# Values right behind scores, turns of probabilities in odd slots, a mask in 64x32 blocks, rope tables one by one

## The chip, the cores and the metric

The kernel runs on one core of a Trainium2 chip. The metric is the device time of one execution in microseconds (us). The engines are TensorE (PE in the profile, its weight loads PEld), VectorE (DVE), ScalarE (ACT), GpSimd (POOL) and SyncE (SP), which issues the transfers. Each engine works through its own queue in order; semaphores tie the queues together.

## The reference

The input is x of 16 sequences x 256 tokens x 128 features, f32. First comes a selective state space block (the first 18% of the span), which the change doesn't touch. Then `x + ffn(layernorm(x))`, where ffn is six layers of local attention and a gated feed-forward part:

```python
for i in range(DEPTH):                       # 6
    x = attn_layer(shift_tokens(x), Wqkv[i], q_scale[i], k_scale[i], Wo[i]) + x
    x = ffn_layer(shift_tokens(x), ln_g[i], ln_b[i], W1[i], b1[i], W2[i], b2[i]) + x
```

The attention has 16 heads of 64. q and k are normalised to length one per head, scaled by a vector, and turned by rotary tables. The sequence is cut in windows of 32 tokens. The queries of a window see its own 32 keys and the 32 before it; of these 64 keys, those later than the query or more than 32 earlier are masked, and the first window of a sequence has no earlier keys. Softmax over the 64 keys, then the weighted sum of v, then the product with Wo. The feed-forward part is a layer norm, a product to 2 x 341, `a * gelu(gate)`, and a product back to 128.

## The kernel before

All is f32, except the mask and its identity (bf16). x stays in SBUF, turned (features on partitions), in `xT`.

**Slots.** A layer is 64 slots (`LAYER`). Slot k begins unit k: one sequence has four units, two chunks of 128 tokens times q and k. Every engine runs the same function `layer_slot(l, k)` for each slot, with its own part of the work, and each kind of work has a lag: unit t's rope is in slot t, its turn to `qT` or `kT` in slot t + 2. A layer's tail overlaps with the next layer's head, in a loop over layers. `step_at` gives work that comes once in two slots, a step: half the heads of a sequence. There are 192 steps. Scores have lag 6, sums of the exponentials 7, turn of the probabilities (`LAG_PTURN`) 8, values (`LAG_VALUES`) 9, output product (`LAG_OUT`) 10, addition to x 11. So scores, turn of probabilities and output product lie in even slots, values and addition in odd ones. `group_at` gives feed-forward work, once per eight slots (48 groups in all): mean 19, variance 21, up products 23, 25 and 27, down product 29; all in odd slots. In k % 8 these are: 3 the mean and up products; 5 the variance and the down product; 7 up products with two Gelus; 1 up products with one Gelu.

**TensorE, one slot** (`layer_slot`, L1225 to L1297), in this order: the unit's projection into `QK` (L1130); feed-forward products (L1215, L1222, L1238, L1250); scores of a step (L1158, L1164); first turn of unit k - 2, `transposes(..., 0)` (L1002); values (L1188); in even slots the projection of v into `VOB` (L1136); turn of the probabilities into `OB` (L1002); second turn of unit k - 2; in odd slots the projection of v; output product into `VOB` (L1196). A line `trb L1002` in the profile is a first or second turn, `ob L1002` the turn of the probabilities.

**The mask** is written into the PSUM tile `SC` by two bf16 products of the full array, an identity times the mask repeated over the head pairs (L1158); the scores are added on top (L1164), each a block of 64 rows by 32 columns of the array. Values are blocks of 64 by 64 (L1188), 128 matmul instructions per step, as the scores.

**What TensorE waits for.** Both turns of a unit go through one PSUM bank, `TRB`: the second waits until ScalarE has copied the first away (`tr_evac`, L633). Mean, variance, v and output product all use `VOB`: the output product waits for ScalarE's copy of v (`v_ready`, L640) and of the values (`o_evac`, L656); v in an odd slot waits for VectorE's use of the mean (`ln_xc`, L956), ScalarE's logarithm (`ln_log`, L703), or the addition to x (L919).

**ScalarE, one slot** (L680): squares of the unit (L619); table load and Gelus (L686, L678); copy of the first turn; the feed-forward norm's square, logarithm and exponential (L698, L703, L705); copy of the values (`out_evac`, L656); in even slots copy of v (L640); copy of the turned probabilities (`probs_evac`, L649); copy of the second turn; in odd slots copy of v; table load back (L721); in slots k % 4 = 2 staging of x (L663 to L671); exponentials of a step (L644); the unit's norms (L623, L626).

**VectorE, one slot** (L934): addition to x (L919), sums (L910), rope (L889, L890), maxima and subtraction (L902, L905), feed-forward operations (L956, L925, L931), sums of squares (L895, L897), norm (L976, L979). At a layer's first slot `layer_tables` makes the four rope tables (L878).

**GpSimd**: divides the probabilities (L514), adds the halves of the rope (L500), scales a unit (L507). **SP** loads weights and shifts copies of v by half a block (`vs` from `vn`).

Of the kernel before, what the change touches and what calls it, by code (L numbers as in the profile page):

```python
# [12 lines left out]
P = 128  # L13
# [3 lines left out]
CHUNKS = SEQ // P  # L17
D_INNER, D_STATE, CONV = 256, 16, 4
MT = D_INNER // P
DEPTH, HEADS, HEAD, WINDOW = 6, 16, 64, 32  # L20
# [17 lines left out]


LAG_TURN, LAG_V, LAG_SHIFT = 2, 3, 4  # L40
LAG_SCORES, LAG_SUM, LAG_PTURN, LAG_VALUES, LAG_OUT, LAG_ADD = 6, 7, 8, 9, 10, 11
LAG_STAGE, LAG_MEAN, LAG_VAR, LAG_NORMED = 17, 19, 21, 22
LAG_UP, LAG_DOWN = (23, 25, 27), 29
TURN = 32
# [52 lines left out]
def build(nc, t, out):  # L97
# [3 lines left out]
    with ctx:  # L101
# [5 lines left out]
        def sem(name, credits=0):  # L107
            s = ctx.enter_context(nc.semaphore(name))
            credit[name] = credits
            return (s, credits)  # L110

        def item(e, s, n):

            e.wait_ge(s[0], n + (1 + s[1]))
# [183 lines left out]
        vproj_done = sem("vproj_done", 2 * UNITS)  # L298
        v_ready = sem("v_ready", 1)
        vs_in = sem("vs_in")  # L300
        s_done = sem("s_done", 2 * STEPS)
        mx_done = sem("mx_done")
        sub_done = sem("sub_done", 1)
# [226 lines left out]
        def _(act_e):  # L530
# [142 lines left out]
            def gelu(group, n, m, done, col):  # L673
                h0, hn = HT[m]
                act_e.wait_ge(up_done[0], n * (2 * NHT) + done + 1)
                if m == 0:
                    slot(act_e, y_done, n)
                A(gl(group, m)[0:hn], SC[0:hn, col:col + 512], ACT.Gelu, bias=lpar[0:hn, 3 + NHT + m:4 + NHT + m]).then_inc(gelu_done[0], 1)  # L678

            def layer_slot(l, k):  # L680
                unit = unit_at(l, k, 0)
                if unit:
                    squares(*unit)
                up0, up1 = group_at(l, k, LAG_UP[0]), group_at(l, k, LAG_UP[1])
                if up0 or up1:
                    act_e.preload_act_table(ACT.Gelu)  # L686
                if up0:
                    gelu(*up0, 0, 0, 0)
                    gelu(*up0, 1, 1, 512)
                if up1:  # L690
                    gelu(*up1, 2, 2, 0)
                at_ = unit_at(l, k, LAG_TURN)
                if at_:
                    turned(*at_, 0)
                at_ = group_at(l, k, LAG_MEAN)
                if at_:
                    item(act_e, ln_xc, at_[1] + 2 * GROUPS)
                    A(sq2[0], xc[0], ACT.Square).then_inc(ln_sq[0], 1)  # L698
                at_ = group_at(l, k, LAG_VAR)
                if at_:  # L700
                    item(act_e, ln_var, at_[1] + 2 * GROUPS)
                    item(act_e, ln_out, at_[1] + (2 * GROUPS - 1))
                    A(rstd[0], bank[2][:], ACT.Ln, bias=eps[:, 0:1]).then_inc(ln_log[0], 1)  # L703
                    item(act_e, ln_log, at_[1] + 2 * GROUPS)
                    A(rstd[0], rstd[0], ACT.Exp, scale=-0.5).then_inc(ln_rstd[0], 1)  # L705
                at_ = step_at(l, k, LAG_VALUES)
                if at_:
                    out_evac(*at_)
                value = v_at(l, k)
                if value and k % 2 == 0:  # L710
                    v_evac(value[0], value[3:], value[2])
                at_ = step_at(l, k, LAG_PTURN)
                if at_:
                    probs_evac(*at_)
                at_ = unit_at(l, k, LAG_TURN)
                if at_:
                    turned(*at_, 1)
                if value and k % 2:
                    v_evac(value[0], value[3:], value[2])
                if up0 or up1:  # L720
                    act_e.preload_act_table_set(EXP_LN_SET)  # L721
                if k % UNITS == 2:
                    at_ = unit_at(l, k, -2)
                    if at_:
                        stage_x(at_[1], at_[2], (k + 2) // UNITS % BATCH, l + (k + 2) // LAYER)
                    at_ = group_at(l, k - 1, LAG_STAGE)
                    if at_:
                        stage_norm(*at_)
                at_ = step_at(l, k, LAG_SCORES)
                if at_:  # L730
                    exps(*at_)
                if unit:
                    norms(*unit)
# [17 lines left out]
        def _(dve):  # L751
# [119 lines left out]
            item(dve, mo_used, GROUPS - 1)  # L871
            plain_norm(GROUPS, xT)

            def layer_tables(l, layer):

                for c in range(CHUNKS):
                    for tab, base, sc in ((tab_q, base_q, scale_q), (tab_k, base_k, scale_k)):
                        V.tensor_tensor(tab[:, c], base[:, c], sc[:, ds(layer, 1), :].to_broadcast([P, 2, HEAD]), ALU.mult) \  # L878
                            .then_inc(tabs_done[0], 1)

            def rope(U, B, u, c, j):

# [51 lines left out]
            def layer_slot(l, k):  # L934
                at_ = step_at(l, k, LAG_ADD)
                if at_:
                    add_x(*at_, (k - LAG_ADD) // UNITS % BATCH * SEQ)
                at_ = step_at(l, k, LAG_SUM)
                if at_:
                    sums(*at_)  # L940
                unit = unit_at(l, k, 0)
                if unit and k % LAYER == 0:
                    layer = l + k // LAYER
                    if k:
                        item(dve, roped, unit[0] * 2 + -1)
                    layer_tables(l, layer)
                    item(dve, tabs_done, layer * (2 * CHUNKS) + (2 * CHUNKS - 1))
                if unit:
                    rope(*unit)
                at_ = step_at(l, k, LAG_SCORES)  # L950
                if at_:
                    maxima(*at_)
                at_ = group_at(l, k, LAG_MEAN)
                if at_:
                    item(dve, ln_mean, at_[1] + 2 * GROUPS)
                    V.tensor_tensor(xc[0], xs2.rearrange("p s t -> p (s t)"), bank[2][:], ALU.subtract).then_inc(ln_xc[0], 1)  # L956
                at_ = group_at(l, k, LAG_UP[1])
                if at_:
                    hidden(*at_, 0, 3, 512)
                at_ = group_at(l, k, LAG_UP[2])  # L960
                if at_:
                    hidden(*at_, 1, 4, 0)
                    hidden(*at_, 2, 5, 512)
                at_ = group_at(l, k, LAG_DOWN)
                if at_:
                    add_y(*at_)
                if unit:
                    square_sums(*unit)
                at_ = group_at(l, k, LAG_NORMED)
                if at_:  # L970
                    if at_[0] == 0:
                        layer = l + (k - LAG_NORMED) // LAYER
                        V.tensor_copy(lpar[:], lpar_all[:, ds(layer, 1), :].rearrange("p o n -> p (o n)")).then_inc(lpar_done[0], 1)
                        item(dve, lpar_done, layer)
                    item(dve, ln_rstd, at_[1] + 2 * GROUPS)
                    V.scalar_tensor_tensor(out=xc[0], in0=xc[0], scalar=lpar[:, 0:1], in1=rstd[0], op0=ALU.mult, op1=ALU.mult) \  # L976
                        .then_inc(ln_aff[0], 1)
                    item(dve, ln_aff, at_[1])
                    V.tensor_scalar(xnT[:, at_[0] * GROUP:at_[0] * GROUP + GROUP], xc[0], lpar[:, 1:2], None, ALU.add).then_inc(ln_out[0], 1)  # L979

            dve.wait_ge(lpar_in[0], N_LPAR)
            dve.wait_ge(cleared[0], 2)
            item(dve, ln_out, 2 * GROUPS - 1)
            layer_slots(dve, layer_slot)
            item(dve, x_next, DEPTH * GROUPS - 1)
# [10 lines left out]
        def _(pe):  # L996
# [147 lines left out]
            def scores(s, B, u, j, n, up0, up1, up2, down):  # L1144
# [9 lines left out]
                    pe.wait_ge(hid_done[0], up2[1] * NHT + 3)  # L1154
                if down:
                    item(pe, x_next, down[1])
                for h in range(2):
                    MM(SC[:, 512 * h:512 * h + 512], lhsT=ident16[:], rhs=mask[:, :].unsqueeze(1).to_broadcast([P, STEP_PAIRS, 2 * SPAN]),  # L1158
                       start=True, stop=True)
                for a in range(STEP_PAIRS):  # L1160
                    for b, g, t0 in windows():
                        for h in range(2):
# [62 lines left out]
            def layer_slot(l, k):  # L1225
# [30 lines left out]
                at_ = step_at(l, k, LAG_SCORES)  # L1256
                if at_:
                    scores(*at_, *(group_at(l, k - 1, lag) for lag in LAG_UP), group_at(l, k - 1, LAG_DOWN))
                turned = unit_at(l, k, LAG_TURN)
                if turned:  # L1260
                    transposes(*turned, 0)
                at_ = step_at(l, k, LAG_VALUES)
                if at_:
                    values(*at_)
                value = v_at(l, k)
                if value and (k - LAG_V) % LAYER == 0:
                    pe.wait_ge(wqkv_in[2][0], (l + (k - LAG_V) // LAYER) * 16 + 16)
# [49 lines left out]
def constants():  # L1317
# [5 lines left out]

    i, k = np.arange(P)[:, None], np.arange(2 * SPAN)[None, :]
    inside = (k % SPAN >= i % WINDOW) & (k % SPAN <= i % WINDOW + WINDOW)
    inside &= (i >= WINDOW) | (k >= SPAN) | (k % SPAN >= WINDOW)
    out["mask"] = np.where(inside, 0.0, MASKED).astype(bf)

    sel = np.zeros((P, 2 * D_STATE, P))
# [36 lines left out]
```

## Time and profile before

| | |
|---|---|
| three runs | 3815.24, 3816.27 (median), 3817.18 us |
| profiled execution | 3817.41 us, span 3815.5 us |
| PE busy | 3549.1 us, 93% |
| DVE busy | 3112.5 us, 82% |
| ACT busy | 2650.5 us, 69% |
| POOL busy | 2420.8 us, 63% |
| transfers | 120.05 MB, some 11% of the 16 DMA engines |

A timeline row is a run of like instructions: start, the time from the first start to the last end, and their count. Matmuls are pipelined, so runs overlap, and the distance from one row's start to the next row's start is what a run takes of TensorE's time. An f32 product is recorded as two matmuls. A share of busy time is an average over all stages.

### The profile page before, as it was taken

The page shows a single profiled execution, that of the slowest core. Times are in us where ns is not written, and L with a number is a line of the kernel's source. Part 1 is how long each engine was busy: PE and PEld are TensorE (multiplying, and loading weights), DVE is VectorE, ACT ScalarE, POOL GpSimd, SP SyncE. Part 2 cuts the span into 40 slices and gives each one's busy share as a digit, 9 for nine tenths or more (in the row PEclk, how much of TensorE's full clock was granted, in tenths as well). Part 3 has the DMA queues.
Part 4 walks back from the last instruction along what each step waited for, and adds up shares of the span by engine and source line. Part 5 has one row for each costly group of instructions (what it writes and reads, how often), then busy time and mean ns, then how long its engine had stood idle before and what let it go on. Part 6 is the DMA issues. An engine that isn't in the chain of part 4 may idle for free.

```text
span 3815.5 us, 146379 instructions
## 1 busy us (share of the span) xinstructions
PE 3549.1 (93%) x60112; PEld 2231.2 (58%) x60128; DVE 3112.5 (82%) x4377; ACT 2650.5 (69%) x4972; POOL 2420.8 (63%) x2197
## 2 busy tenths in 40 slices
PE   5667676899999999999999999999999999999997
PEld 2222222466666666666666666666666666666664
DVE  4899998888888888888878888878888788888884
ACT  3545454677777777777777777777777777777775
POOL 0356555776666666666666666666666666666661
PEclk9889899999999999999999999999999999999999
DMA  3000000010111111111111111111111111111101
GB/s 78 0 0 0 0 0 0 26 37 28 33 35 48 37 33 32 32 48 37 37 33 32 43 43 35 30 32 32 48 41 34 32 32 48 37 37 29 33 28 38
DMA packets 64418, 120.05 MB, mean 31 GB/s; under 512 B 18196, under 2 KB 35986, under 8 KB 63634
## 3 DMA queue, kind: packets, MB, share of 16 engines
q1 hardware_dynamic: 63762, 110.70, 10.0%
q8 instruction: 485, 7.95, 0.9%
q14 instruction: 171, 1.40, 0.1%
HBM read 20.50 MB, written 2.10 MB: 6 GB/s over the span
## 4 chain that ended last, share of the span: by engine, by line
PE 79%; issue 2%; DVE 2%; ACT 1%; POOL 0%; DMA 0%; ACTq 0%; POOLq 0%; DVEq 0%; SPq 0%
PE qk L1130 17%; PE trb L1002 10%; PE ob L1188 10%; PE vob L1196 8%; PE vob L1136 8%; PE sc L1164 7%; PE sc L1215 6%; PE ob L1002 4%; PE sc L1222 3%; PE sc L1158 2%; PE vob L1238 1%; PE vob L1250 1%; DVE arena L889 0%; DVE ssq L895 0%; DVE arena L890 0%
## 5 line engine op out<-in xcount | busy, mean ns | idle before, releaser
L507 POOL TENSOR_TENSOR arena<-arena,rnorm 128x512 f32<-128x512 f32 x768 | 785.2, 1044 | 930.0 <-ACT rnorm L626 929.5
L500 POOL TENSOR_TENSOR arena<-arena 128x512 f32<-128x512 f32 x768 | 962.8, 1275 | 35.9 <-DVE arena L890 35.9
L633 ACT ACTIVATE arena<-trb 128x512 f32<-128x512 f32 x768 | 462.6, 602 | 441.6 <-PE trb L1002 441.6
L1130 PE MATMUL qk<-wqkv,xs 128*128 128x512 f32 x1536 | 729.4, 597 | 16.3 <-issue 9.2
L889 DVE TENSOR_TENSOR arena<-qk,tab_q 128x512 f32<-128x512 f32 x384 | 263.3, 686 | 455.0 <-ACT arena L619 447.6
L483 POOL TENSOR_TENSOR arena<-arena 128x512 f32<-128x512 f32 x256 | 300.0, 1182 | 346.4 <-DVE arena L859 333.8
L1002 PE MATMUL trb<-ident,arena 128*128 128x128 f32 x3072 | 482.3, 280 | 9.8 <-ACT arena L633 7.3
L1130 PEld LDWEIGHTS qk<-wqkv,xs 128*128 128x128 f32 x1536 | 292.7, 191 | 309.1 <-issue 291.7
L895 DVE TENSOR_REDUCE ssq<-arena 128x16 f32<-128x1024 f32 x384 | 463.7, 1207 | 0.0
L619 ACT ACTIVATE arena<-qk 128x512 f32<-128x512 f32 x768 | 426.8, 588 | 45.0 <-PE qk L1130 28.1
L1002 PEld LDWEIGHTS trb<-ident,arena 128*128 128x128 f32 x3072 | 346.7, 141 | 140.1 <-issue 88.3
L514 POOL TENSOR_TENSOR arena<-arena,rinv 128x512 f32<-128x512 f32 x384 | 392.6, 1044 | 23.1 <-DVE rinv L912 23.1
L1188 PE MATMUL ob<-arena 64*64 64x32 f32 x24576 | 397.2, 220 | 0.0
L1188 PEld LDWEIGHTS ob<-arena 64*64 64x64 f32 x24576 | 375.9, 135 | 33.9 <-issue 33.9
L1136 PE MATMUL vob<-wqkv,xs 128*128 128x512 f32 x768 | 393.8, 594 | 1.1 <-DVE arena L956 1.1
L1196 PE MATMUL vob<-arena,wo 128*128 128x256 f32 x1536 | 363.6, 380 | 1.3 <-ACT arena L656 1.3
L1164 PEld LDWEIGHTS sc<-arena 64*32 64x32 f32 x24576 | 254.7, 105 | 84.3 <-issue 84.2
L1196 PEld LDWEIGHTS vob<-arena,wo 128*128 128x128 f32 x1536 | 276.9, 190 | 31.2 <-issue 1.4
L1164 PE MATMUL sc<-arena 64*32 64x64 f32 x24576 | 287.0, 225 | 1.5 <-issue 1.1
L1215 PE MATMUL sc<-xnT,w 128*128 128x512 f32 (+1 forms) x576 | 271.1, 593 | 5.3 <-DVE xnT L979 2.2
L640 ACT ACTIVATE arena<-vob 128x512 f32<-128x512 f32 x384 | 232.9, 607 | 51.1 <-PE vob L1136 50.8
L1090 PE MATMUL sc<-arena,ident 128*128 128x512 f32 x512 | 257.3, 624 | 8.8 <-POOL arena L483 6.8
(139 smaller groups left out, 5879.6 us busy)
## 6 DMA issues: line engine op xcount, KB each, us to landing
arena<-arena SPq DMA_DIRECT2D x192, 384.0 KB, 3.2
arena<-arena SPq DMA_DIRECT2D x192, 64.0 KB, 3.0
wqkv<-in_L_ffn_Wqkv SPq DMA_DIRECT2D x18, 512.0 KB, 4.6
wo<-in_L_ffn_Wo SPq DMA_DIRECT2D x6, 512.0 KB, 4.0
arena<-in_L_attn_x SPq DMA_DIRECT2D x8, 256.0 KB, 2.9
out<-arena SPq DMA_DIRECT2D x8, 256.0 KB, 2.2
w<-in_L_ffn_W SPq DMA_DIRECT2D x6, 341.0 KB, 2.9
arena<-in_sel SPq DMA_DIRECT2D x1, 1024.0 KB, 5.0
```

What stands on the lines that cost most here:

```text
L500: nc.gpsimd.tensor_tensor(ts[c * 2 + j][:, heads], tu[:, 0, heads], tu[:, 1, heads], ALU.add).then_inc(summed[0], 1)
L507: nc.gpsimd.tensor_tensor(part, part, rnorm[j][:, 8 * h:8 * h + 8].unsqueeze(2).to_broadcast([P, 8, HEAD]), ALU.mult) \
L619: A(sq[j][:, cols], QK[:, cols], ACT.Square).then_inc(sq_ready[0], 1)
L633: A((qT, kT)[j][u][:, 4 * h:4 * h + 4, at_col:at_col + P], TRB.rearrange("p (a t) -> p a t", a=4), ACT.Copy) \
L895: V.tensor_reduce(ssq[j][:], sq[j].rearrange("p (h e) -> p h e", h=HEADS), op=ALU.add, axis=AX.X).then_inc(ssq_done[0], 1)
L1002: return MM(out_, lhsT=in_, rhs=ident[0:k, 0:k], is_transpose=True, **kw)
L1130: MM(QK[:, 512 * h:512 * h + 512], lhsT=xs[u][:, c * P:(c + 1) * P], rhs=wqkv[:, col:col + 512], start=True, stop=True) \
L1136: MM(VOB[:, :], lhsT=xs[u][:, c * P:(c + 1) * P], rhs=wqkv[:, col:col + STEP_COLS], start=True, stop=True).then_inc(vproj_done[0], 1)
L1164: last = MM(SC[32 * g:32 * g + 32, col:col + SPAN], lhsT=qT[u][d, STEP_PAIRS * j + a, t0:t0 + WINDOW], rhs=kT[u][d, STEP_PAIRS * j + a, t0 ...
L1188: last = MM(OB[d, col:col + WINDOW], lhsT=v[keys, g // 2, (2 * a + h) * HEAD:(2 * a + h + 1) * HEAD], rhs=probT[keys, h, a, g * WINDOW:(g ...
L1196: last = MM(VOB[:, 0:SEQ], lhsT=wo[:, STEP_PAIRS * j + a, :], rhs=oT[:, a, :], start=a == 0, stop=a == STEP_PAIRS - 1)
L1215: MM(SC[0:hn, 512 * b:512 * b + 512], lhsT=w1[:, col:col + hn], rhs=rhs, start=True, stop=True).then_inc(up_done[0], 1)
```

## The change

Turn of the probabilities has lag 9 and values lag 10: the turn now lies in odd slots, the values in even ones, where TensorE does them right behind the scores of a later step and ahead of the first turn. ScalarE's copy of the values comes accordingly right behind the squares and Gelus, ahead of the copy of the first turn. The mask is written by eight products of 64x32 blocks, behind a new semaphore increment; the mask constant is repeated in both halves of the partitions. The four rope tables of a layer are made one at a time, behind the last units that use the old one, and each of the first four units of a layer waits for its own.

```diff
-LAG_SCORES, LAG_SUM, LAG_PTURN, LAG_VALUES, LAG_OUT, LAG_ADD = 6, 7, 8, 9, 10, 11
+LAG_SCORES, LAG_SUM, LAG_PTURN, LAG_VALUES, LAG_OUT, LAG_ADD = 6, 7, 9, 10, 10, 11
...
@@ ScalarE
                 if up1:
                     gelu(*up1, 2, 2, 0)
+                at_ = step_at(l, k, LAG_VALUES)
+                if at_:
+                    out_evac(*at_)
                 at_ = unit_at(l, k, LAG_TURN)
                 if at_:
                     turned(*at_, 0)
...
-                at_ = step_at(l, k, LAG_VALUES)
-                if at_:
-                    out_evac(*at_)
                 value = v_at(l, k)
...
@@ VectorE
-            def layer_tables(l, layer):
-
-                for c in range(CHUNKS):
-                    for tab, base, sc in ((tab_q, base_q, scale_q), (tab_k, base_k, scale_k)):
-                        V.tensor_tensor(tab[:, c], base[:, c], sc[:, ds(layer, 1), :].to_broadcast([P, 2, HEAD]), ALU.mult) \
-                            .then_inc(tabs_done[0], 1)
+            def layer_table(layer, c, j):
+
+                tab, base, sc = (tab_q, tab_k)[j], (base_q, base_k)[j], (scale_q, scale_k)[j]
+                V.tensor_tensor(tab[:, c], base[:, c], sc[:, ds(layer, 1), :].to_broadcast([P, 2, HEAD]), ALU.mult).then_inc(tabs_done[0], 1)
...
-                if unit and k % LAYER == 0:
-                    layer = l + k // LAYER
-                    if k:
-                        item(dve, roped, unit[0] * 2 + -1)
-                    layer_tables(l, layer)
-                    item(dve, tabs_done, layer * (2 * CHUNKS) + (2 * CHUNKS - 1))
+                if unit and k % LAYER < UNITS:
+                    dve.wait_ge(tabs_done[0], (l + k // LAYER) * UNITS + k % LAYER + 1)
...
+                ahead = unit_at(l, k, 1)
+                if ahead and not isinstance(l, int) and LAYER - UNITS <= (k - 1) % LAYER:
+                    item(dve, roped, ahead[0] * 2 + 1)
+                    layer_table(l + 1, ahead[3], ahead[4])
...
@@ TensorE
-                for h in range(2):
-                    MM(SC[:, 512 * h:512 * h + 512], lhsT=ident16[:], rhs=mask[:, :].unsqueeze(1).to_broadcast([P, STEP_PAIRS, 2 * SPAN]),
-                       start=True, stop=True)
+                pe.sem_inc(s_open[0], 1)
+                for g in range(4):
+                    for h in range(2):
+                        d, pick = slice(64 * h, 64 * h + 64), 64 * h + (WINDOW if g else 0)
+                        MM(SC[32 * g:32 * g + 32, 512 * h:512 * h + 512], lhsT=ident16[d, pick:pick + WINDOW],
+                           rhs=mask[d, :].unsqueeze(1).to_broadcast([64, STEP_PAIRS, 2 * SPAN]), start=True, stop=True, skip_group_check=True)
...
                 if at_:
                     scores(*at_, *(group_at(l, k - 1, lag) for lag in LAG_UP), group_at(l, k - 1, LAG_DOWN))
+                at_ = step_at(l, k, LAG_VALUES)
+                if at_:
+                    values(*at_)
                 turned = unit_at(l, k, LAG_TURN)
                 if turned:
                     transposes(*turned, 0)
-                at_ = step_at(l, k, LAG_VALUES)
-                if at_:
-                    values(*at_)
...
-    inside &= (i >= WINDOW) | (k >= SPAN) | (k % SPAN >= WINDOW)
+    inside &= (i % SPAN >= WINDOW) | (k >= SPAN) | (k % SPAN >= WINDOW)
```

## Rows read from the trace of the kernel before

**Rows 1.** Of the page: busy time of the engines; shares of the chain of waits

```profile
PE 3549.1 (93%) x60112; PEld 2231.2 (58%) x60128; DVE 3112.5 (82%) x4377; ACT 2650.5 (69%) x4972; POOL 2420.8 (63%) x2197
...
PE 79%; issue 2%; DVE 2%; ACT 1%; POOL 0%; DMA 0%; ACTq 0%; POOLq 0%; DVEq 0%; SPq 0%
```

**Rows 2.** One stretch of 2800 us in the layers: time, busy per engine, TensorE clock, DMA

```profile
900.00:3700.00 2800.00, 2789.58 (x53631) 1857.29 (x53632) 2286.88 (x3290) 2093.62 (x4007) 1919.47 (x1742) 1.00 0.13 36
```

**Rows 3.** Waits of TensorE in that stretch: us in total, times, longest

```profile
PE qk L1130 <- issue: 9.2, 4, 2.5
```

**Rows 4.** TensorE in order of time, an even slot: start us, us, instructions

```profile
2007.92 1.88 PE L1130 MATMUL qk<-wqkv,xs 128*128 128x512 f32 x4
2009.64 0.59 PE L1158 MATMUL sc<-mask,ident 128*128 128x512 bf16 x2
2010.16 1.48 PE L1164 MATMUL sc<-arena 64*32 64x64 f32 x128
2011.58 0.65 PE L1002 MATMUL trb<-ident,arena 128*128 128x128 f32 x4
2012.07 1.02 PE L1136 MATMUL vob<-wqkv,xs 128*128 128x512 f32 x2
2012.93 1.04 PE L1002 MATMUL ob<-ident,arena 128*128 128x128 f32 x8
2013.80 0.60 PE L1002 MATMUL trb<-ident,arena 128*128 128x128 f32 x4
2014.24 1.89 PE L1196 MATMUL vob<-arena,wo 128*128 128x256 f32 x8
2015.97 1.88 PE L1130 MATMUL qk<-wqkv,xs 128*128 128x512 f32 x4
```

**Rows 5.** TensorE in order of time, the odd slot that follows

```profile
2020.26 0.60 PE L1002 MATMUL trb<-ident,arena 128*128 128x128 f32 x4
2020.79 2.07 PE L1188 MATMUL ob<-arena 64*64 64x32 f32 x128
2022.79 0.66 PE L1002 MATMUL trb<-ident,arena 128*128 128x128 f32 x4
```

**Rows 6.** Groups by shape: busy us, mean ns | idle before us

```profile
L889 DVE TENSOR_TENSOR arena<-qk,tab_q 128x512 f32<-128x512 f32 x384 | 263.3, 686 | 455.0 <-ACT arena L619 447.6 <-POOL arena L500 7.4
...
L1158 PE MATMUL sc<-mask,ident 128*128 128x512 bf16 x384 | 114.2, 379 | 0.2 <-DVE hid_last L925 0.2
...
L878 DVE TENSOR_TENSOR tab_k<-base_k,scale_k 128x128 f32<-128x128 f32 x12 | 3.3, 279 | 0.0
```

**Rows 7.** TensorE in order of time, in the tail of the last layer

```profile
3769.91 2.07 PE L1188 MATMUL ob<-arena 64*64 64x32 f32 x128
3773.28 1.97 PE L1196 MATMUL vob<-arena,wo 128*128 128x256 f32 x8 [1.30 <-ACT arena L656]
```

**Rows 8.** ScalarE in order of time, the same place in the tail

```profile
3772.05 1.08 ACT L656 ACTIVATE arena<-ob 128x512 f32<-128x512 f32 x2 [1.34 <-PE ob L1188]
```

**Rows 9.** TensorE in order of time, start of an odd slot with two Gelus

```profile
2049.27 1.88 PE L1130 MATMUL qk<-wqkv,xs 128*128 128x512 f32 x4
```

**Rows 10.** ScalarE in order of time, that odd slot and its end

```profile
2051.81 1.28 ACT L686 ACT_TABLE_LOAD   x1
...
2054.26 0.60 ACT L633 ACTIVATE arena<-trb 128x512 f32<-128x512 f32 x1
2055.44 1.09 ACT L656 ACTIVATE arena<-ob 128x512 f32<-128x512 f32 x2 [0.59 <-PE ob L1188]
2056.41 0.60 ACT L633 ACTIVATE arena<-trb 128x512 f32<-128x512 f32 x1
2056.89 0.62 ACT L640 ACTIVATE arena<-vob 128x512 f32<-128x512 f32 x1
```

**Rows 11.** VectorE in order of time, the odd slot of rows 5

```profile
2022.15 0.67 DVE L956 TENSOR_TENSOR arena<-xs,vob 128x512 f32<-128x512 f32 x1
```

**Rows 12.** ScalarE in order of time, the even slot of rows 4

```profile
2014.58 0.62 ACT L633 ACTIVATE arena<-trb 128x512 f32<-128x512 f32 x1
```

More of the change, by code:

```diff
@@ L300, in build @@
         vs_in = sem("vs_in")
+        s_open = sem("s_open")
         s_done = sem("s_done", 2 * STEPS)
@@ L982, in _ @@
             dve.wait_ge(cleared[0], 2)
+            for c in range(CHUNKS):
+                for j in range(2):
+                    layer_table(0, c, j)
             item(dve, ln_out, 2 * GROUPS - 1)
```

## The prediction

> **What bounds the kernel now.** I read the page's totals first. TensorE is busy 93% of the span, the next engine 82%, and 79% of the chain that ended last is TensorE [rows 1]. A share over all stages says little, so the second view is one stretch inside the layers. There TensorE is busy 2789.6 of 2800 us at a granted clock of 1.00, which is the 2.4 GHz level; VectorE has 2286.9 and ScalarE 2093.6 [rows 2]. The third view, the waits of TensorE there, has 9.2 us in four waits of up to 2.5 us [rows 3]. So the layers are a gapless stream of TensorE: whatever shortens it is gained in full, and every new wait in it is paid in full. The other engines' slack matters only as distance to the next TensorE instruction that waits for them. That distance is read from the timelines, as start-to-start times (busy times overlap). Two slots make one step; there are 192 steps, in 48 groups of eight slots.
>
> An even slot, from S = 2007.92, issues projection 1.72, mask 0.52, scores 1.42, first turn 0.49, values projection (v) 0.86, probabilities' turn 0.87, second turn 0.44, output product 1.73: 8.05 us [rows 4]. In the odd slot first turn 0.53 and values 2.00 follow the feed-forward products [rows 5].
>
> **Gain 1, the mask.** Two blocks of 512 bf16 columns take 0.59 in all and one takes 0.379, so the second starts 0.21 behind the first; 0.52 less two of these leaves 0.09 before the first 64x32 block [rows 4, 6]. The same 0.09 is the difference between the turn ahead of values (0.53) and the one ahead of the output product (0.44) [rows 4, 5]. After the change the 0.09 stands ahead of the mask, and eight blocks on eight parts of the array stream the 512 columns. No row has such a block. Below: side by side, 0.21, no less, for one part must still stream 512 columns. Above: the four blocks of one half one after another, 0.86. The nearest row is the 128 score blocks on the same eight parts: 1.42/128 = 11 ns each, of 64 f32 columns, where 512 take 0.43 and so 64 take 54 ns [rows 4]. They clearly run side by side, and I take 0.21. Mask and entry go from 0.52 to 0.31: 0.21 x 192 = 41 us. The upper end would make it a loss of 0.43 x 192 = 83 us.
>
> The Trainium skill, "TensorE: Matmul & The Clock Gate", Measured speedup vs the span model, gives 6.32x for nine packed blocks, some 70% of nine. By that, as an estimate, the eight blocks would take about 0.30 and the gain would be 18 us less; the score rows show overlap but do not separate 70% from 100%.
>
> **Gain 2, one change of block shape fewer.** Values are no longer entered from a full-array turn, so 0.09 goes: x 190 steps = 17 us. What stands between the last score block and the first value block no row shows: nothing (then 0.05 more gained) up to one more 0.09 (nothing gained). I take the exit that the turn behind scores has now, already inside 1.42.
>
> The Trainium skill, "TensorEngine Tiling (Array Packing)", Key Properties, says a change of tiling mode drains the array; the 0.09 at every entry agrees. 64x32 to 64x64 would be such a change, which is the value taken.
>
> **No gain or loss.** The table edit moves 24 operations of about 0.28 us on VectorE [rows 6]. VectorE idles 447.6 us in all before the q rope, waiting for ScalarE's squares, which hides them at either place [rows 6]; without that cover they would cost 24 x 0.28 = 7 us. The added semaphore increment ahead of the mask: the same kind stands ahead of values, whose entry costs the same 0.09 as the scores' without one, so nothing (at most 0.1 x 192 = 19 us). Turning probabilities one slot later frees `prob` one slot later, but the subtraction that rewrites it stands a slot behind that turn. Value buffers come free one slot later; four steps apart, the copy that waits for them comes in the slot after. No DMA moves; SP's shifts hang on that copy and have a slot more before values.
>
> **Loss 1, behind values in every even slot.** Now the probabilities' turn and the second turn, 1.31 us, stand between v and the output product; afterwards only the second turn, 0.44. Count from the start of values, B. Ideal: first turn B+2.00, v B+2.49, second turn B+3.35, output product B+3.79. ScalarE must first copy the two halves of values, for it is now first in its queue. It starts 0.07 behind values' end (3769.91 + 2.07 to 3772.05) [rows 7, 8], B+2.14, and a copy follows the other every 0.485 (2055.44 to 2056.41 for two), each ending 0.60 after its start [rows 10]. So: copy of the first turn B+3.11 to B+3.71, copy of v B+3.59 to B+4.20 (v itself ends B+2.49 + 1.02 = B+3.51). The second turn needs the bank that the first copy frees (`tr_evac`), the output product the bank of v (`v_ready`). TensorE restarts 0.15 behind such a copy (3773.13 to 3773.28), its block then 0.08 longer (1.97 against 1.89) [rows 4, 7, 8]. Output product in effect B+4.42 against 3.79: 0.63. Without restart cost it is 0.41. Queued behind it: the next projection, so the whole stream. I take 0.63 x 189 = 119 us.
>
> **Loss 2, odd slots whose length was the cover.** They lose values (2.00) and gain a turn (0.87). From the slot's start T, first turn after projection and up products 3.44, second turn due at T+3.44+0.44+0.87 = 4.75.
> - With two Gelus, T = 2049.27: table load 2051.81, copy of the first turn 2054.26 to 2054.86, T+5.59 [rows 9, 10]. All of it hangs on this slot's projection, so it stays. The second turn waits until 5.69 (0.1 taken for the restart): 0.94.
> - With one Gelu the copy is 0.57 earlier (two Gelus and a load fill 2051.81 to 2054.26, the load 1.28): T+5.02, so 0.37.
> - With the mean, T = 2015.97: v overwrites the mean's bank and waits for the subtraction, which ends 2022.82, T+6.85 [rows 4, 11]. It hangs on ScalarE's second copy in the slot before, now 1.39 ahead of T (2014.58) [rows 12], after the change 1.65 (second turn's copy B+4.49, T at B+6.14), so T+6.59. v is due at T+4.29+0.44+0.87+0.44 = 6.04 [rows 4, 5]: 0.65 with the restart.
> - With the variance: about 0.1, v against the logarithm.
>
> Some 46 of the 48 groups have these slots full: (0.94 + 0.37 + 0.65 + 0.1) x 46 = 95 us. With the restarts at nothing: 0.84, 0.27, 0.55 and 0 make 76.
>
> **The sum.** Gains 41 + 17 = 58; losses 119 + 95 = 214; net +156. The profiled execution took 3817.4 (its span 3815.5), so 3973; the median of the runs is 1.1 lower: 3972 us. In slots: eight took 64.1, they would take 67.3. Own range: losses 77 + 76 give 3911; mask at 0.30, and a second shape change's 17 give 4007.
>
> **Rivals.**
> 1. Only Loss 1: ScalarE's and VectorE's chains in the short odd slots move forward with them. For: with the long even slot both engines have more time in all. Against: the table load hangs on the slot's own projection. 3816 - 58 + 119 = 3877. Chance 0.12.
> 2. The mask blocks of one half run one after another. For: no row has bf16 blocks of 512 columns there. Against: 11 ns a score block. 3972 + 124 = 4096. Chance 0.07.
> 3. Faster: the copies behind values don't hold TensorE. Place: `v_ready` and `tr_evac` in the even slot; price 0.63; it decides where the waits of a step sum to under 58/192 = 0.30 us. For: the stream has no wait there now. Against: v ends 0.28 before the output product is due and its copy lasts 0.6. 3816 - 58 = 3758. Chance 0.08.
> 4. Gains and losses cancel, with half of each loss. 3816. Chance 0.03.
>
> The forecast has 0.70. The range 3865 to 4012 takes in rival 1. A measurement of this kernel tells 0.2% (8 us) from no change: faster 0.08, same 0.03, slower 0.89.
>
> **What would show it.** In the waits of TensorE, the second turn and the output product waiting for ScalarE's copies, about 0.4 to 0.6 in each even slot, and a wait of v for VectorE's subtraction once a group; these rows hardly exist now. Mask to scores start-to-start 0.21 with eight blocks. Values right behind scores in the timeline, at the old 2.00. Wrong if: the output product starts within 0.1 of the second turn's end; a slot of two Gelus lasts under 6.2 us; or the mask block lasts over 0.4.

## The result and the profile after

The changed kernel takes 4456.6 us (median of 4 runs, 4448.9 to 4460.4) against 3816.7: 1.167 times as long, interval 1.166 to 1.169. The prediction said 3972: it had the direction right and the size wrong, +156 us forecast and +640 measured. The profiled execution's span is 4454.8 us.

The page after, its totals, the chain of waits, two groups by shape and the queue that brings instructions:

```profile
PE 3800.4 (85%) x61280; PEld 2348.5 (53%) x61280; DVE 3097.2 (70%) x4377; ACT 2648.5 (59%) x4972; POOL 2418.3 (54%) x2197
...
q8 instruction: 492, 8.06, 0.8%
...
PE 60%; issue 15%; ACT 8%; DVE 3%; POOL 0%; ACTq 0%; DMA 0%; DVEq 0%; POOLq 0%; SPq 0%
...
L1193 PE MATMUL ob<-arena 64*64 64x32 f32 x24576 | 458.8, 224 | 282.9 <-issue 280.8
...
L1138 PE MATMUL vob<-wqkv,xs 128*128 128x512 f32 x768 | 479.1, 711 | 11.4 <-DVE arena L951 11.3
```

"issue" went from 2% of the chain [rows 1] to 15%. It is time in which TensorE does nothing and the profile shows nothing that it waits for. 280.8 us of it lie inside the values (now L1193). The last row is another loss: one matmul of the v product lasts 711 ns on average, where it lasted 594.

The waits of TensorE between 1000 and 4300 us (total, times, longest); before, the same view of the layers had a single row of 9.2 us [rows 3]:

```profile
PE ob L1193 <- issue: 249.7, 160, 2.9
PE trb L1004 <- ACT arena L634: 67.9, 164, 0.8
PE qk L1132 <- issue: 10.7, 4, 2.8
PE vob L1138 <- DVE arena L951: 8.7, 25, 0.5
PE vob L1201 <- ACT arena L641: 7.8, 27, 0.3
```

TensorE in order of time, an even slot whose clock stays at the upper level, answering to [rows 4]:

```profile
2109.54 1.88 PE L1132 MATMUL qk<-wqkv,xs 128*128 128x512 f32 x4
2111.35 0.41 PE L1163 MATMUL sc<-mask,ident 64*32 64x512 bf16 x8
2111.58 1.46 PE L1169 MATMUL sc<-arena 64*32 64x64 f32 x128
2112.98 1.00 PE L1193 MATMUL ob<-arena 64*64 64x32 f32 x52
2115.26 1.35 PE L1193 MATMUL ob<-arena 64*64 64x32 f32 x76 [1.27 <-issue]
2116.54 0.66 PE L1004 MATMUL trb<-ident,arena 128*128 128x128 f32 x4
2117.04 1.02 PE L1138 MATMUL vob<-wqkv,xs 128*128 128x512 f32 x2
2118.35 0.65 PE L1004 MATMUL trb<-ident,arena 128*128 128x128 f32 x4 [0.29 <-ACT arena L634]
2118.84 1.99 PE L1201 MATMUL vob<-arena,wo 128*128 128x256 f32 x8
2120.67 1.88 PE L1132 MATMUL qk<-wqkv,xs 128*128 128x512 f32 x4
```

The mask takes 0.23 us from start to start and values begin 1.40 behind the scores, as worked out. Then values stop after 52 of their 128 instructions for more than a microsecond, with no semaphore in between. Behind them second turn and output product are late, nearly as forecast: from the first turn to the output product it is 2.30 us, where the forecast had 2.42 (B+2.00 to B+4.42) and 1.79 without waits. The slot lasts 11.13 us; forecast 9.6. ScalarE's copies in that slot (of the first turn, of v):

```profile
2117.62 0.60 ACT L634 ACTIVATE arena<-trb 128x512 f32<-128x512 f32 x1
2118.10 0.62 ACT L641 ACTIVATE arena<-vob 128x512 f32<-128x512 f32 x1
```

They end at 2118.22 and 2118.72; the second turn and the output product start 0.13 and 0.12 behind. Nearly all of the delay is the second turn's: the output product starts 0.49 behind it, where it started 0.44 behind it before [rows 4].

TensorE in an odd slot with two Gelus, and the start of the next:

```profile
2083.05 1.88 PE L1132 MATMUL qk<-wqkv,xs 128*128 128x512 f32 x4
2084.76 1.88 PE L1220 MATMUL sc<-xnT,w 128*128 128x512 f32 x4
2086.48 0.60 PE L1004 MATMUL trb<-ident,arena 128*128 128x128 f32 x4
2086.92 1.04 PE L1004 MATMUL ob<-ident,arena 128*128 128x128 f32 x8
2088.76 0.66 PE L1004 MATMUL trb<-ident,arena 128*128 128x128 f32 x4 [0.80 <-ACT arena L634]
2089.25 1.02 PE L1138 MATMUL vob<-wqkv,xs 128*128 128x512 f32 x2
2090.11 0.59 PE L1132 MATMUL qk<-wqkv,xs 128*128 128x512 f32 x1
```

The second turn starts 5.71 us into the slot; forecast 5.69. The slot lasts 7.06; forecast 6.99.

**Where the values stop.** Three things can be counted in the trace. First, in program order of TensorE's instructions, the 180 stops of over 0.6 us in scores and values lie multiples of 256 apart, nearly always 512, 768 or 1280; a third are off by one, four by seven. Second, the queue `q8 instruction` brings one piece of 16 KB at a time, 492 in all, which is a piece for some 256 instructions of TensorE. In the slot above one starts at 2112.92 and lands at 2113.88, and values go on at 2115.26, 1.37 us behind the landing; over all of these stops this distance is 1.2 to 1.6 us, median 1.38. Third, from the instruction 256 ahead of a stop's end to that end it is 3.5 us in the median, and 3.1 to 4.3 in nine of ten. So in this kernel a piece becomes usable some 3.5 us after TensorE has entered the piece before it. Scores and values are 256 instructions each (128 weight loads, 128 matmuls) at 5.5 and 7.2 ns apiece: a piece is used up in 1.7 us, and 1.8 are missing. There are 175 stops of over 0.25 us inside values, together 315 us.

In the kernel before, eight such stops stand inside scores, 3.2 us in all. The only one of over 0.6 us from start to start is in the tail, where a slot's other work is gone (TensorE in order of time; 0.58 us of it idle):

```profile
3752.88 0.76 PE L1164 MATMUL sc<-arena 64*32 64x64 f32 x52
3754.22 0.99 PE L1164 MATMUL sc<-arena 64*32 64x64 f32 x76 [0.58 <-issue]
```

**The clock.** Another even slot, in which TensorE's clock fell; then the two slots and the odd one behind them as windows (stretch, length, busy per engine, granted clock, DMA):

```profile
2131.73 1.83 PE L1193 MATMUL ob<-arena 64*64 64x32 f32 x112
2135.10 0.43 PE L1193 MATMUL ob<-arena 64*64 64x32 f32 x16 [1.53 <-issue]
2135.47 0.66 PE L1004 MATMUL trb<-ident,arena 128*128 128x128 f32 x4
2135.96 1.80 PE L1138 MATMUL vob<-wqkv,xs 128*128 128x512 f32 x2
2137.56 1.06 PE L1004 MATMUL trb<-ident,arena 128*128 128x128 f32 x4
```

```profile
2109.54:2120.67 11.13, 9.57 (x287) 6.92 (x286) 6.33 (x9) 6.94 (x14) 4.64 (x5) 1.00 0.08 22
2128.30:2139.88 11.58, 10.05 (x283) 6.83 (x282) 7.75 (x11) 6.40 (x14) 5.86 (x6) 0.85 0.05 12
2139.88:2147.86 7.98, 7.98 (x35) 4.72 (x33) 5.92 (x9) 3.06 (x8) 6.54 (x6) 1.00 0.16 47
```

In the second slot v lasts 1.80 instead of 1.02: the lower of the two levels, 1.2 GHz (a granted clock of 0.50 from 2136.07 to 2139.48), behind a stop in the values that ended at 2135.10. Of the 102 stretches at the lower level in the layers, 95 begin inside a stop or within 3 us behind one, which together is a quarter of the layers' time. Of the 176 even slots that have every kind of work, 86 run at the upper level throughout and last 11.22 us on average, with 1.49 us of stops; 90 have a stretch at the lower level and last 12.96, with 1.85 us of stops.

### The profile page after: what moved, and what is told of

It is laid out like the page before. It is cut to its first block, busy times and chain, and to the rows that moved or that the text cites. A ratio compares the mean times of both kernels' runs of the same rounds, so it can differ in the third digit from the quotient of the medians.

```text
span 4454.8 us, 148907 instructions
## 1 busy us (share of the span) xinstructions
PE 3800.4 (85%) x61280; PEld 2348.5 (53%) x61280; DVE 3097.2 (70%) x4377; ACT 2648.5 (59%) x4972; POOL 2418.3 (54%) x2197
## 4 chain that ended last, share of the span: by engine, by line
PE 60%; issue 15%; ACT 8%; DVE 3%; POOL 0%; ACTq 0%; DMA 0%; DVEq 0%; POOLq 0%; SPq 0%
PE qk L1132 14%; PE ob L1193 10%; PE vob L1138 8%; PE trb L1004 8%; PE vob L1201 7%; PE sc L1169 6%; PE sc L1227 3%; ACT arena L634 2%; PE sc L1163 1%; PE ob L1004 1%; PE sc L1220 1%; PE vob L1243 1%; ACT L687 1%; DVE arena L889 1%; DVE rsum L909 1%
## 5 line engine op out<-in xcount | busy, mean ns | idle before, releaser
L1193 PE MATMUL ob<-arena 64*64 64x32 f32 x24576 | 458.8, 224 | 282.9 <-issue 280.8
L657 ACT ACTIVATE arena<-ob 128x512 f32<-128x512 f32 x384 | 208.4, 595 | 787.9 <-PE ob L1193 787.9
L1004 PE MATMUL trb<-ident,arena 128*128 128x128 f32 x3072 | 549.1, 306 | 89.1 <-ACT arena L634 80.2
L1004 PEld LDWEIGHTS trb<-ident,arena 128*128 128x128 f32 x3072 | 387.1, 154 | 427.2 <-issue 357.6
L1193 PEld LDWEIGHTS ob<-arena 64*64 64x64 f32 x24576 | 417.9, 139 | 311.9 <-issue 294.8
L1138 PE MATMUL vob<-wqkv,xs 128*128 128x512 f32 x768 | 479.1, 711 | 11.4 <-DVE arena L951 11.3
L918 DVE TENSOR_TENSOR xT<-vob,xT 128x256 f32<-128x256 f32 x192 | 81.5, 424 | 574.6 <-PE vob L1201 574.4
L1201 PE MATMUL vob<-arena,wo 128*128 128x256 f32 x1536 | 408.0, 411 | 13.9 <-ACT arena L641 9.0
L1201 PEld LDWEIGHTS vob<-arena,wo 128*128 128x128 f32 x1536 | 297.0, 205 | 83.0 <-issue 35.9
L1169 PEld LDWEIGHTS sc<-arena 64*32 64x32 f32 x24576 | 279.5, 105 | 18.0 <-issue 7.3
```

The source lines that it names most:

```text
L1004: return MM(out_, lhsT=in_, rhs=ident[0:k, 0:k], is_transpose=True, **kw)
L1138: MM(VOB[:, :], lhsT=xs[u][:, c * P:(c + 1) * P], rhs=wqkv[:, col:col + STEP_COLS], start=True, stop=True).then_inc(vproj_done[0], 1)
L1169: last = MM(SC[32 * g:32 * g + 32, col:col + SPAN], lhsT=qT[u][d, STEP_PAIRS * j + a, t0:t0 + WINDOW], rhs=kT[u][d, STEP_PAIRS * j + a, t0 ...
L1193: last = MM(OB[d, col:col + WINDOW], lhsT=v[keys, g // 2, (2 * a + h) * HEAD:(2 * a + h + 1) * HEAD], rhs=probT[keys, h, a, g * WINDOW:(g ...
L1201: last = MM(VOB[:, 0:SEQ], lhsT=wo[:, STEP_PAIRS * j + a, :], rhs=oT[:, a, :], start=a == 0, stop=a == STEP_PAIRS - 1)
```

## The experiments

Two theories stood. F: the stops are the supply of instructions; they need more than 256 short instructions in a row. S: they come from values standing directly behind scores with another block shape. A third, C, puts the loss on ScalarE's copies and the clock, and M, in one expectation, on the mask blocks. The first four kernels ran together; their time before was 3820.3 us. The old order and values first have four runs each, the tables alone eleven, and every other kernel a single one; stops are counted in the trace of one run each.

**The old order, mask blocks and single tables kept.**

```diff
-LAG_..., LAG_PTURN, LAG_VALUES, LAG_OUT, LAG_ADD = 6, 7, 9, 10, 10, 11
+LAG_..., LAG_PTURN, LAG_VALUES, LAG_OUT, LAG_ADD = 6, 7, 8, 9, 10, 11
# and values, out_evac back in their old places
```

> The changed kernel with the old order put back (turn of probabilities lag 8, values lag 9 in odd slots behind the first turn, copy of the values in its old place); mask blocks and single rope tables stay. Theory F (instruction supply): TensorE's instructions arrive in pieces of 256; a piece is ready about 3.5 us after TensorE enters the one before, so 256 score instructions with 256 value instructions right behind run dry at a piece's boundary. Here 256 short instructions stand alone, so no gap over 0.6 us inside values, and the mask's gain stays: 0.21 x 192 = 41 us, 3775 us (3768 to 3788). Rival M (the mask blocks are the cause): even slots stay over 10 us, 4200 us or more. Rival S (the cause is values standing directly behind scores with another block shape): 3775 too.

Measured 3787.6 us (3784.3 to 3791.7), ratio 0.991, interval 0.989 to 0.993: 33 us faster than before. Its TensorE, in an even slot:

```profile
2010.79 1.88 PE L1132 MATMUL qk<-wqkv,xs 128*128 128x512 f32 x4
2012.60 0.41 PE L1163 MATMUL sc<-mask,ident 64*32 64x512 bf16 x8
2012.83 1.46 PE L1169 MATMUL sc<-arena 64*32 64x64 f32 x128
2014.22 0.66 PE L1004 MATMUL trb<-ident,arena 128*128 128x128 f32 x4
```

From the projection to the first turn it is 3.43 instead of 3.66 [rows 4]. The mask blocks don't cause the loss (M falls), and this kernel beats both others. The whole loss is in the order.

**Half of the values.**

```diff
-                for a in range(STEP_PAIRS):        # values
+                for a in range(STEP_PAIRS // 2):
```

> The changed kernel with only half of the value products (pairs 0 and 1 of 4; leaves the other half of the attention's output wrong). 384 short instructions in a row in place of 512. Theory F: a whole piece of 256 lies inside the row only where its boundary falls in the first 128, so the gap is in about half of the 192 steps (80 to 115, against 175 now), each still some 1.8 us; time about 3972 - 0.93 x 190 = 3795, plus 95 x 1.8 = 171, plus up to 60 for the clock: 3940 to 4030. Rival S (change of shape right behind scores): a gap in every step, 4456 - 176 = 4280. Rival C (the copies of ScalarE and the lower clock, no supply): no gaps inside values, 3800 to 3900.

Measured 4018.1 us, inside F's range. Stops inside values: 96, together 159 us, where there were 175. The half that F worked out from 384 against 256 is met; a stop at every meeting of scores and values (S) and no stop (C) fall.

**Scores twice in the kernel before.**

```diff
-                for a in range(STEP_PAIRS):        # scores
+                for a in 2 * list(range(STEP_PAIRS)):
```

> The kernel before with every score product issued twice (scores come out doubled), so 512 short instructions of one shape stand in a row; order, mask and values as before. Theory F: a gap inside the scores in nearly every step, 3.5 - 1.4 = 2.1 us: 3816 + 192 x 1.35 (259) + 190 x 2.1 (399) = 4475 us (4350 to 4600). Rivals S and C: no gap, 3816 + 259 = 4075 us.

Measured 4502.2 us, inside F's range; the rivals had 4075. TensorE in one of its even slots (the view begins inside the row), its waits, and the instruction queue:

```profile
2099.77 1.59 PE L1164 MATMUL sc<-arena 64*32 64x64 f32 x140
2103.52 0.86 PE L1164 MATMUL sc<-arena 64*32 64x64 f32 x65 [2.15 <-issue]
```

```profile
PE sc L1164 <- issue: 306.7, 166, 3.7
```

```profile
q8 instruction: 677, 11.09, 1.0%
```

These are 169 stops inside scores, 344 us in all, with no values near, no change of shape and no late copy: neither S nor C can explain them. The 192 x 256 instructions more bring 192 pieces more (677 against 485).

**Values at the head of the even slot.**

```diff
 def layer_slot(l, k):
+    values(*at_)        # TensorE; on ScalarE out_evac ahead of the squares
     unit(*unit_)
     scores(...)
-    values(*at_)
```

> The changed kernel with values (and ScalarE's copy of them) moved to the head of the even slot, ahead of the unit's projection: 1.72 + 0.31 us of long products now stand between the 256 value and the 256 score instructions. Theory F: gaps shrink to under 0.3 us, even slots to about 9.7, and the time falls to what the waits of the prediction leave: 3985 us (3950 to 4050). Rival S: 3985 as well. Rival C (values in an even slot cost what they cost wherever they stand in it): over 4300 us.

Measured 4265.4 us (4262.4 to 4269.4), ratio 1.117, interval 1.115 to 1.119. F and S said 3985, C over 4300: a miss, and nearer to C. The waits of TensorE between 1000 and 4000 us:

```profile
PE ob L1193 <- issue: 69.6, 45, 4.4
PE ob L1193 <- ACT arena L650: 57.2, 82, 0.8
PE sc L1169 <- issue: 36.5, 32, 2.0
PE vob L1201 <- ACT arena L641: 31.8, 149, 0.3
```

Two things were left out of the expectation. Values now wait for ScalarE's copy of the turned probabilities from the slot before. And 52 stops in values and 48 in scores, together 133 us, are left of the changed kernel's 175 and 11, though no row has more than 256 short instructions. F said gaps under 0.3 us, and that is wrong.

The trace shows where F is too simple. At the stops of over 0.6 us the time from the instruction 256 ahead to the stop's end is no longer 3.5 us but 5.4 in the median and up to 11.8. The distance from a piece's landing to going on is still 1.2 to 1.6 us; it is the fetch that starts late, 2.9 us in the median behind the entry into the piece before, where it was 1.0 in the changed kernel, and often only when TensorE is already in the short row. So the start of a fetch is not a fixed time behind that entry. What sets it stays open, and so does the part of the 280 us over the expectation that stops and waits don't fill.

The next four ran together, before at 3817.1 us.

**Half of scores and half of values, new and old order.** The two edits of above, once in the changed kernel and once in the old order with mask blocks.

> The changed kernel with half of the score products and half of the value products (leaves the attention's output wrong): values still right behind scores, but 256 short instructions in all, no longer than one piece. Theory F: hardly a gap, the clock stays at its upper level, and the time is the forecast's: 3972 less 0.66 x 190 for scores and 0.93 x 190 for values, 3670 us (3640 to 3710), with the output product waiting for the copies 0.6 us in each even slot. Theory C (clock and copies make the loss, supply little): the same loss as now, 4456 - 302 = 4154 us.

> The old order with mask blocks (the kernel e1_old_order) with the same half of scores and values left out. 3788 - 302 = 3486 us, and some 50 us of waits in odd slots, since values' 1.0 us less there uncovers the copy of the first turn (0.7 us with two Gelus) and v's wait for the mean's subtraction: 3510 to 3550. The difference to e8_half_both_new, 130 us (100 to 170), is what the reordering costs without the supply. Theory C: the difference is some 600 us.

Measured 3734.2 and 3692.6 us; both are above their ranges. In the new order there are 11 stops, 6 us, where 175 were: 256 short instructions in a row, though scores and values still touch. The lower clock goes with them: 8 stretches of it in the layers against 102. The even slot lasts 8.03 us in the median; the forecast less the work left out, 9.60 - 1.59, is 8.01. TensorE there (second turn and output product late by the copies):

```profile
2100.30 0.66 PE L1004 MATMUL trb<-ident,arena 128*128 128x128 f32 x4
2100.79 1.02 PE L1138 MATMUL vob<-wqkv,xs 128*128 128x512 f32 x2
2102.14 0.65 PE L1004 MATMUL trb<-ident,arena 128*128 128x128 f32 x4 [0.32 <-ACT arena L634]
2102.63 1.99 PE L1201 MATMUL vob<-arena,wo 128*128 128x256 f32 x8
```

The difference of the two is 42 us, not 130. Both expectations were too low: with so much work gone TensorE waits for other engines in the odd slots. In the new order the four odd slots of a group last 0.7 us longer than in the changed kernel; in the old order with half of the work these waits of TensorE between 1000 and 3600 us are new (with all products no wait of that view for VectorE or ScalarE stands there):

```profile
PE sc L1220 <- DVE xnT L978: 68.6, 42, 1.9
PE trb L1004 <- ACT arena L634: 49.5, 42, 1.3
PE vob L1138 <- DVE arena L951: 19.1, 42, 0.5
```

So the pair shows that stops and lower clock all but vanish with the row of short instructions, and doesn't show what the order alone costs.

**The projection of v between scores and values; then first turn and v between.**

```diff
     scores(...)
+    v_unit(...)         # second kernel: transposes(*turned, 0), then v_unit(...)
     values(*at_)
```

> The changed kernel with the projection of v (0.86 us, four instructions) between scores and values, ScalarE's copy of v ahead of that of the values. Theory F: the gap inside values shrinks by the 0.86, from 1.8 to 0.9 us, in as many steps. The waits behind values grow, since both turns now follow them directly: second turn 1.3 and output product little, so 3972 + 140 + 190 x 0.8 = 4260 us (4180 to 4340). Theory S (values directly behind scores): no gap at all, since they no longer stand next to each other.

> The changed kernel with the first turn and the projection of v (together 1.3 us, 12 instructions) between scores and values; ScalarE's copy of the values behind its copy of v. Theory F: where a piece's boundary falls in values, the gap is what 3.5 us leave after 1.7 us of short instructions and 1.3 of long ones, 0.4 to 0.6 us (1.8 with nothing between, 0.76 with v alone). The output product waits for the copies of the values, about 1.0 us in each even slot: 3972 + 190 x (1.0 - 0.6) + 175 x 0.5 = 4135 us, some 50 more for the lower clock (4080 to 4240). Theory S (only direct neighbours stall): no gap, as for e5, where it failed.

Measured 4407.6 and 4175.4 us (beside the second the kernel before took 3821.8). What stands between, the stops of over 0.25 us inside values, and their mean from start to start:

```
nothing (changed kernel)    0.00 us    175 stops    1.80 us each
v                           0.86 us    172 stops    0.76 us each
first turn and v            1.35 us    135 stops    0.58 us each
```

The stop shrinks with what is put in between, by somewhat more than its length for v and less for both, and does not vanish with the neighbourhood: S falls. The first time came out above its range, the second inside: both turns now follow values and wait for copies (the waits row of that kernel, whole span):

```profile
PE trb L1004 <- ACT arena L634: 272.6, 282, 2.7
```

**The tables alone, in the kernel before.**

> The kernel before with the rope tables one by one as the only edit. VectorE waits at a layer's first slots anyway: 3820 us, within 0.1% of before. The difference to e1_old_order is then the mask's: some 33 of the 41 us forecast. A rival: the tables cost or give 8 us, and the mask gives 41 or 25.

Measured 3821.3 us, ratio 1.0008, interval 0.9999 to 1.0017. No effect that can be measured, at most 0.2%. The 33 us of the old order with mask blocks are then the mask's, within some 8 us.

## Why the prediction was wrong, point by point

**The bound.** Right: TensorE's stream was full, and what came into it was paid in full.

**Gain 1.** Right in kind, a little smaller than forecast: 33 us against 41. Mask and entry fell by 0.23 us in the median even slot (8.05 to 7.82), forecast 0.21; the eight blocks take 0.23, nearer to the 0.21 taken than to the 0.30 estimated beside it. Some 4 us went to short stops in scores (13 with 7 us, before 8 with 3), and some 5 to three even slots with a stretch at the lower clock (9.50 against 7.88).

**Gain 2.** Right as far as the trace shows: values start 1.40 behind scores, where the turn started 1.42 behind them, so no second change of shape is paid there.

**Tables.** Right.

**Loss 1.** The copies hold TensorE as forecast: 8.03 measured against 8.01 in the kernel with half of scores and values, and there 2.33 us from first turn to output product, forecast 2.42. One of the prediction's signs of being wrong did come, the output product starting within 0.1 of the second turn's end (2118.84 against 2119.01). It was ill chosen: before, too, it starts ahead of that end [rows 4]. The wait lies at the second turn, and the copy of v is done almost in time.

**Loss 2.** Right: in the median the odd slots of a group last 7.06 (two Gelus), 6.47, 7.55 (the mean) and 7.98 us, 29.06 in all. Before they lasted 7.32, 7.32, 8.17 and 9.03; less values and one entry each (4 x 2.09), plus a turn each (4 x 0.87) and the forecast's waits (2.06) that is 29.02.

**What failed** is the second sentence of Loss 1's count, "first turn B+2.00": values were priced at the 2.00 us that they take in [rows 5], standing alone, and "values at the old 2.00" was even given as the sign to look for. An instruction's price was carried from a place where 256 short instructions stand between long products to one where 512 stand together. There they took 3.6 us (2112.98 to 2116.54). No rival held this. The fall of TensorE's share of the chain from 79% to 60%, and the 280.8 us of "issue", are its mark. The prediction also had no term for the clock, and 90 of 176 even slots have a stretch at the lower level.

The sum with what was measured in its place, against the forecast of 3972. Of the 1.74 us between the two kinds of even slots 0.36 are longer stops (1.85 - 1.49), already in the first line, so 1.38 are put down to the clock:

```
forecast                                             3972
stops in values, 175 x 1.80                          +315
lower clock, 1.38 x 90/176 x 190 slots               +134
                                                     4421
measured                                             4456.6
```

36 us are left. Even slots without lower clock are 0.13 us longer than forecast and stops (9.60 + 1.49 against 11.22), which would be 25 us of it if it holds for all; the rest isn't placed. The clock's part is the difference of two kinds of slots of one run, no experiment. Stretches at the lower level in the layers and stops of over 0.25 us inside scores and values, kernel by kernel: 102 with 186 (changed kernel), 54 with 188 (v between), 46 with 169 (scores twice), 33 with 102 (half of values), 29 with 100 (values first), 22 with 151 (first turn and v between), 8 with 11 and 7 with 3 (half of both, new and old order), 6 with 15 (old order), 3 with 3 (tables alone), 2 with 8 (before). Kernels with a hundred stops or more have at least 22 stretches, those with fewer than twenty at most 8; how many stops go with one stretch differs, and what else decides it stays open.

The Trainium skill bears on this in "Runtime: NRT & Kernel Launch", Instruction fetch mechanics: instructions come in blocks of 16 KiB, 256 instructions, and crossing a boundary is "mostly hidden". The block size agrees with the 256 between stops and the 16 KB pieces. The hiding does not hold where 512 of TensorE's short instructions stand together: 1.8 us per stop here. The section also gives TensorE room for 2048 instructions, and a few lines on only two blocks; a reserve of 2048 would have carried it over 512, and the 3.5 us from one piece's start to the next one's use show none.

## What to carry to other kernels

Count instructions, not only microseconds: in these runs a row of TensorE with more than 256 short instructions (weight loads count) ran dry in most places where a piece was used up in under some 3.5 us, and its price in a calmer place did not foretell that. So spread rows of tiny matmuls between long products; here the old order did that. Rows of 256 are no safe limit, as the kernel with values first shows: measure the new place. Before two such rows are put together, look in the profile for "issue" inside one of them: a single 0.58 us in the tail was the warning. And where a copy stands between two products in one PSUM bank, what lay between them was its cover, and moving that away costs the part of the copy that it covered.

## What the runs showed of the hardware that was not expected

TensorE's instructions arrive in pieces of 16 KB (256). At the stops of the changed kernel a fetch takes 1.1 us in the median, the first instruction of it runs 1.2 to 1.6 us after it has landed, and the fetch starts about 1 us after the piece before is entered: 3.5 us in all, or 14 ns per instruction over a piece, where scores alone go at 5.5 ns. In the kernel with values first the fetch starts later (median 2.9 us), and the other two times stay about the same. In that changed kernel 90 of 176 even slots have a stretch at the lower clock; of the same slots before, none has.

Eight bf16 blocks of 64x32 with 512 columns, on eight parts of the array, take 0.23 us together from start to start, about as long as one such product of the full array (0.21 [rows 4, 6]).
